# A mask bias moved from TensorE matmuls to a VectorE pass in an attention, and an expert stage of 71 slots instead of 72

## The chip, the cores and the metric

The kernel runs on one core of one Trainium2 chip. The metric is the device time of one execution in microseconds; before the change it is 3022.76 us, the median of three runs (3021.39 to 3025.53).

## The reference

The model has two layers over an activation x of 8 batches of 512 tokens of 512 numbers (4096 tokens, 32 tiles of 128). Each layer is a cross attention to a context of 77 keys per batch, and a feed-forward part:

```python
x = x + cross_attention_0(context, layernorm(x), mask)   # 16 heads of 32, masked softmax over 77 keys
x = x + bit_linear_ffn(layernorm(x))                     # 8-bit activations, ternary weights, a depthwise conv
x = x + cross_attention_1(layernorm(x), context)         # 16 heads of 64, no mask
x = x + moe(layernorm(x))                                # 8 experts, the best 2 per token
```

In the first attention the scores of a masked key are replaced by -1e20 before the softmax; the mask is an input of [8, 1, 512, 77] and is 0 for the padded keys of a batch. The softmax is taken over energy / sqrt(512). In the last part each token goes to 2 of 8 experts, so there are 8192 rows to be worked on, sorted by expert; an expert computes silu(x W_gate) * (x W_up) with 1024 hidden numbers, and multiplies by W_2.

## The kernel before, in words

The program is a sequence of blocks, each finished by all engines before the next begins: the context's keys and values, the first attention, the feed-forward part, the second attention, the routing, the experts, and the combination. The change touches the second, the fifth to seventh through one constant, and the loop of the sixth.

**The first attention** (`attention0`, from L314) goes over 32 tiles of 128 tokens, one per step, software-pipelined by hand: the order in which each engine does its work is written out in its own loop over steps, and semaphores tie them. Heads are worked in two halves of 8; a half's scores are [128, 2, 4 x 77] in two PSUM banks, 616 numbers per token. In step s TensorE does, in this order: for each half the scores of tile s (`score_half`), the mix of values of tile s - 2 (`mix`), the transposes of tile s + 1's normalized input (`turn`), the output product of tile s - 3 (`output`), and the four groups of transposes of tile s - 1's probabilities (`flip`). `score_half` first writes the mask's bias, 0 or -1e20, into PSUM with two matmuls of an identity against the bias row repeated over four heads (L423, 308 columns each, bf16), and then adds 16 small products of 32 rows against 77 keys (L428, fp32). `mix`, `turn` and the `flip`s share a ring of three PSUM banks that ScalarE empties.

VectorE in a step: `add` of tile s - 4 (the output product added to x at L572 and statistics at L574), then `shift` for both halves of tile s (a maximum per head straight from PSUM, L552, and the subtraction from PSUM into SBUF tile `e`, L556), every fourth step `masks` for the next batch (L545), and `invert` for both halves (the sum of exponentials, L565, and its reciprocal, L567). ScalarE in a step: the copy of the mix (L519), the exponential of half 0 (L502), the copy of the turned input (L497), the exponential of half 1, the normalization of tile s + 2 (L489), and the four copies of flipped probabilities (L510). GpSimd multiplies the exponentials by the reciprocals (L397, two of them per tile), adds the output bias to x (L400), and at tile 8 issues one DMA that fills `sorted_x` with zeros. TensorE may write a half's scores again when `shifted` says that the subtraction of the tile before has been done; and it waits for `bias_made` before the scores of a batch's first tile.

**Routing and experts.** `SLOTS` (L1467) is the number of slots of 128 rows in the sorted scratch arrays `sorted_x` and `sorted_y`: 64 for the 8192 rows and one for each expert, 72. Each expert gets its count of rows rounded up to whole slots, at least one; slots behind the last that is used count as expert 7's and hold zeros. `experts` (from L1797) works on all slots alike. Per slot TensorE makes the gate and up products of half 0 (24 matmuls, L1919), transposes a part of the slot before, makes those of half 1, the output product of the slot before (24 matmuls, L1939), and transposes a part of its own; ScalarE, VectorE and the DMA queue of SyncE follow. `slots` (L1831) writes out slots 0 and 1, loops over 34 pairs, and writes out the last two. GpSimd meanwhile loads and splits the weights of the next experts. Behind the experts, GpSimd gathers each token's two rows from `sorted_y` in the combination.

Of the kernel before, what the change touches and what calls it, by code (L numbers as in the profile page):

```python
# [23 lines left out]
ALU = mybir.AluOpType  # L24
ACT = mybir.ActivationFunctionType
AX = mybir.AxisListType

P = 128
# [285 lines left out]
def attention0(nc, core, keys, values, w):  # L314
# [7 lines left out]
    with ExitStack() as stack:  # L322
# [21 lines left out]
        weights_in = sem("weights_in"); bo_in = sem("bo_in"); mask_in = sem("mask_in")  # L344
        variance_ready = sem("variance_ready"); root_ready = sem("root_ready"); steps = sem("steps")
        xn_made = sem("xn_made"); bias_made = sem("bias_made"); bo_added = sem("bo_added")
        scores_ready = sem("scores_ready"); topped = sem("topped"); shifted = sem("shifted")
        exp_done = sem("exp_done"); summed = sem("summed"); inverted = sem("inverted")
        probs_ready = sem("probs_ready"); unit_ready = sem("unit_ready"); unit_copied = sem("unit_copied")
        out_ready = sem("out_ready"); out_added = sem("out_added"); stats_made = sem("stats_made")  # L350
# [22 lines left out]
        def grouped(a):  # L373

            return a.rearrange("p (g h k) -> p g h k", g=2, h=CH)
# [27 lines left out]
        @block.tensor  # L403
        def _(pe):
            def ring_free(u):
                if u >= len(ring):
                    pe.wait_ge(unit_copied, u - len(ring) + 1)

            def turn(t):
                u = unit["turn", t]  # L410
                pe.wait_ge(xn_made, t + 1)
                ring_free(u)
                for k in range(KD):
                    last = nc.tensor.transpose(bank(u)[:, k * P:(k + 1) * P], xn[:, t % 2, k * P:(k + 1) * P],
                                               core.ident[:, :])
                last.then_inc(unit_ready, 1)

            def score_half(t, half):
                b = t // TPS
                if t >= 1:  # L420
                    pe.wait_ge(shifted, 2 * (t - 1) + half + 1)
                for g in range(2):
                    nc.tensor.matmul(scores[half][:, g, 0:QUARTER], core.ident_bf[:, :],  # L423
                                     bias[:, t, :].unsqueeze(1).broadcast_to([P, CH, KEYS]), start=True, stop=False)
                for c in range(CH):
                    for g in range(2):
                        rows = slice((2 * half + g) * DH, (2 * half + g + 1) * DH)
                        last = nc.tensor.matmul(scores[half][:, g, c * KEYS:(c + 1) * KEYS],  # L428
                                                xn_t[rows, t % 2, c, :], keys[rows, c, b * KEYS:(b + 1) * KEYS],
                                                start=False, stop=(c == CH - 1))  # L430
                last.then_inc(scores_ready, 1)

            def flip(t, q):
                u = unit["flip", t, q]
                pe.wait_ge(probs_ready, 2 * t + q // 2 + 1)
                ring_free(u)
                for c in range(CH):
                    last = nc.tensor.transpose(bank(u)[0:KEYS, c * P:(c + 1) * P],
                                               heads(e[:, t % 2, q // 2, :])[:, q % 2 * CH + c, :], core.ident[:, :])
                last.then_inc(unit_ready, 1)  # L440

            def mix(t):
                u = unit["mix", t]
                pe.wait_ge(unit_copied, unit["flip", t, ROWS_OF - 1] + 1)
                ring_free(u)
                for c in range(CH):
                    for j in range(ROWS_OF):
                        last = nc.tensor.matmul(bank(u)[j * DH:(j + 1) * DH, c * P:(c + 1) * P],
                                                values[:, t // TPS, c * P + j * DH:c * P + (j + 1) * DH],
                                                probs_t[:, t % 2, j * CH + c, :], start=True, stop=True)  # L450
                last.then_inc(unit_ready, 1)

            def output(t):
                pe.wait_ge(unit_copied, unit["mix", t] + 1)
                if t >= 1:
                    pe.wait_ge(out_added, t)
                for c in range(CH):
                    last = nc.tensor.matmul(out[:, :], mixed_t[:, t % 2, c, :], wo[:, c, :],
                                            start=(c == 0), stop=(c == CH - 1))
                last.then_inc(out_ready, 1)  # L460

            turn(0)
            for step in range(NT + 3):
                if step < NT:
                    pe.wait_ge(unit_copied, unit["turn", step] + 1)
                    pe.wait_ge(bias_made, step // TPS + 1)
                    for half in range(2):
                        score_half(step, half)
                if step == 3:
                    pe.wait_ge(weights_in, 16)  # L470
                if 2 <= step < NT + 2:
                    mix(step - 2)
                if step + 1 < NT:
                    turn(step + 1)
                if step >= 3:
                    output(step - 3)
                if 1 <= step <= NT:
                    for q in range(ROWS_OF):
                        flip(step - 1, q)
# [61 lines left out]
        def _(dve):  # L541
# [5 lines left out]

            def shift(t, half):
                raw = scores[half][:, :, 0:QUARTER].rearrange("p g (h k) -> p g h k", h=CH)
                tops = top[:, half, :].rearrange("p (g h) -> p g h", g=2)  # L550
                dve.wait_ge(scores_ready, 2 * t + half + 1)
                nc.vector.tensor_reduce(tops, raw, AX.X, ALU.max).then_inc(topped, 1)  # L552
                dve.wait_ge(topped, 2 * t + half + 1)
                if t >= 2:
                    dve.wait_ge(unit_ready, unit["flip", t - 2, 2 * half + 1] + 1)
                nc.vector.tensor_tensor(grouped(e[:, t % 2, half, :]), raw,  # L556
                                        tops.unsqueeze(3).broadcast_to([P, 2, CH, KEYS]), ALU.subtract
                                        ).then_inc(shifted, 1)

            def invert(t, half):  # L560
                sums = total[:, t % 2, half, :]
# [902 lines left out]
CW = 1024  # L1464
CHUNKS = (KD * 2 * MID + MC * D) // CW

SLOTS = (2 * B * S) // P + EXPERTS  # L1467
ROWS = SLOTS * P


# [326 lines left out]
def experts(nc, core, plan, w, sorted_x, sorted_y):  # L1797
# [5 lines left out]
    with ExitStack() as stack:  # L1803
# [27 lines left out]
        def slots(engine, slot):  # L1831

            slot(0, 0, True, False)
            slot(1, 1, False, False)
            with engine.Fori(1, PAIRS - 1) as pair:
                slot(2 * pair, 0, False, False)
                slot(2 * pair + 1, 1, False, False)
            slot(SLOTS - 2, 0, False, False)
            slot(SLOTS - 1, 1, False, True)

        @block.gpsimd
        def _(pool):
# [46 lines left out]
        def _(sp):  # L1889
# [16 lines left out]

            slots(sp, slot)
            for u in range(2):
                sp.wait_ge(y_out[u], 16 * PAIRS)

        @block.tensor
        def _(pe):
# [52 lines left out]
        def _(act):  # L1965
# [11 lines left out]
            def slot(s, u, first, last):  # L1977
                gates(s, 0)
                gates(s, 1)
                if not first:  # L1980
                    out_copy(s - 1, 1 - u)

            slots(act, slot)
            out_copy(SLOTS - 1, 1)

        @block.vector
        def _(dve):
# [139 lines left out]
```

## Time and profile before

| | us |
|---|---|
| median of three runs | 3022.76 (3021.39 to 3025.53) |
| the profiled execution's own time | 3018.94 |
| its span, first to last instruction | 3017.2 |
| first attention, from its first instruction to the last of TensorE's output products | 97.4 to 426.3 |
| experts, first product to last output copy | 1732.1 to 2918.6 |

TensorE's mean granted clock over the span is 0.919 of 2.4 GHz. In the rows, PE is TensorE's matmuls, PEld its weight loads, DVE is VectorE, ACT is ScalarE, POOL is GpSimd and SP is SyncE; a line of the timeline merges like instructions (the xN at its end) and gives the start, the time from the first start to the last end, the line and operation, and in brackets the engine's idle time before it. Matmul ends are modelled, so a busy PE is not a PE at its peak; the starts of weight loads are the better marks of its pace.

### The profile page before, as it was taken

To read this page: it belongs to the slowest core of one execution; us is meant where nothing else is said; L and a number is where in the kernel's file an instruction comes from. 1 tells how busy PE (TensorE), PEld (TensorE's weight loads), DVE (VectorE), ACT (ScalarE), POOL (GpSimd) and SP (SyncE) were. 2 spreads that over 40 slices of the span, in tenths; PEclk is the share of its full clock that TensorE was granted. 3 is DMA by queue.
4 is the path that set the end of the run, shared out by engine and by line. 5 is a ranking of instruction groups with operands and counts; after the bars stand their busy time and mean duration, and the time that the engine had idled before them with its cause. 6 is when DMAs were issued, how large, how long until landed. Compare 5 with 4: busy or idle time off the path is not lost. (4 is left out here: it accounts for less than half of the span.)

```text
span 3017.2 us, 45376 instructions
## 1 busy us (share of the span) xinstructions
PE 2468.1 (82%) x15846; PEld 1309.2 (43%) x16027; DVE 1620.3 (54%) x2256; ACT 1015.7 (34%) x1664; POOL 972.8 (32%) x803
## 2 busy tenths in 40 slices
PE   8799964566666699999982099999999999999960
PEld 5566631222222265556551044444444444444430
DVE  4566668898998465656656332242433424332235
ACT  2355535778885444444343211111111111111100
POOL 0243322677776211111103600060533505320026
PEclk9899986888887899999996599999999999999985
DMA  6350010000000200000024501141322413221128
GB/s 232 117 219 34 2 57 0 1 0 1 0 0 0 73 10 10 14 10 10 6 72 141 198 25 35 33 112 35 104 77 79 115 35 102 79 64 33 35 77 275
DMA packets 154415, 190.30 MB, mean 63 GB/s; under 512 B 100070, under 2 KB 103142, under 8 KB 153782
## 3 DMA queue, kind: packets, MB, share of 16 engines
q1 hardware_dynamic: 128933, 98.44, 11.1%
q0 software_dynamic: 25360, 90.21, 9.2%
q8 instruction: 81, 1.33, 0.2%
q14 instruction: 41, 0.33, 0.0%
HBM read 101.77 MB, written 67.96 MB: 56 GB/s over the span
## 5 line engine op out<-in xcount | busy, mean ns | idle before, releaser
L1919 PE MATMUL e_gate_up<-weights,e_x_t 128*128 x3382 | 760.7, 379 | 122.6 <-DMA e_x_t<-sorted_x 118.7
L1919 PEld LDWEIGHTS e_gate_up<-weights,e_x_t 128*128 128x128 bf16 x3456 | 332.6, 98 | 494.2 <-issue 121.1
L1992 DVE TENSOR_TENSOR e_mid<-e_gate,e_gate_up 128x512 f32<-128x512 f32 x144 | 99.0, 688 | 605.5 <-ACT e_gate L1969 605.5
L1939 PE MATMUL e_out<-weights,e_mid_t 128*128 x1692 | 382.8, 379 | 3.0 <-DVE e_mid_t L2005 1.1
L1969 ACT ACTIVATE e_gate<-e_gate_up 128x512 f32<-128x512 f32 x144 | 86.0, 598 | 721.7 <-PE e_gate_up L1919 721.7
L1939 PEld LDWEIGHTS e_out<-weights,e_mid_t 128*128 128x128 bf16 x1728 | 169.1, 98 | 204.8 <-issue 1.2
L708 POOL TENSOR_TENSOR a_e<-a_e,a_total 128x616 f32<-128x616 f32 x64 | 76.5, 1216 | 451.5 <-DVE a_total L960 451.5
L1135 POOL TENSOR_TENSOR f_shared<-f_shared 128x512 f32<-128x512 f32 x128 | 180.8, 1413 | 125.4 <-DVE f_shared L1413 125.4
L1205 PE MATMUL f_out<-f_w,hidden 128*128 128x512 f16 x512 | 141.9, 404 | 95.1 <-ACT hidden L1307 94.5
L1124 POOL TENSOR_TENSOR hidden<-hidden,f_up_row 128x512 f32<-128x512 f32 x128 | 178.7, 1407 | 86.6 <-ACT f_up_row L1336 86.6
L1873 POOL TENSOR_TENSOR e_token<-e_token 1x1 f32<-1x1 f32 x6 | 1.1, 183 | 632.3 <-PE e_out L1939 632.3
L2005 DVE COPY e_mid_t<-e_mid_flip 128x1024 bf16<-128x1024 bf16 x144 | 98.9, 688 | 180.0 <-PE e_mid_flip L1929 179.4
L736 PE MATMUL a_ring<-a_xn_t,a_wq 128*128 128x512 bf16 x752 | 168.6, 381 | 7.5 <-issue 6.7
L1184 PE MATMUL f_product<-f_xq_t,f_w 128*128 128x512 bf16 x489 | 144.0, 423 | 35.5 <-DVE f_padded L1381 22.3
L790 PE MATMUL a_out<-a_wo,a_mixed_t 128*128 128x512 bf16 x737 | 164.3, 379 | 4.5 <-issue 3.0
L1413 DVE SCALAR_TENSOR_TENSOR f_shared<-f_padded,f_conv_w,f_shared 128x512 f32<-128x512 f32 x128 | 152.2, 1191 | 12.9 <-ACT f_shared L1290 12.5
L1880 POOL TENSOR_TENSOR weights<-raw_weights,weights 128x1024 bf16<-128x1024 f32 x72 | 155.6, 2162 | 6.1
L1975 ACT ACTIVATE e_y_rows<-e_out 128x512 f32<-128x512 f32 x72 | 43.0, 597 | 340.4 <-PE e_out L1939 340.4
L2037 POOL DMA_INDIRECT o_y<-sorted_y,plan_rows x64 | 67.9, 1060 | 276.6 <-PEq L2023 257.4
L397 POOL TENSOR_TENSOR a_e<-a_e,a_total 128x616 f32<-128x616 f32 x64 | 76.4, 1215 | 192.3 <-DVE a_total L567 192.3
L1998 DVE TENSOR_TENSOR e_mid_parts<-e_mid,e_mid_parts 128x512 bf16<-128x512 f32 x144 | 128.5, 892 | 5.0
L930 DVE SCALAR_TENSOR_TENSOR a_query<-a_ring,a_bq,a_query 128x512 bf16<-128x512 f32 x64 | 48.0, 751 | 142.8 <-ACT a_query L847 142.8
(233 smaller groups left out, 3985.3 us busy)
## 6 DMA issues: line engine op xcount, KB each, us to landing
raw_weights<-in_w POOLq DMA_DIRECT2D x72, 512.0 KB, 4.0
sorted_x<-a_zero_row POOLq DMA_DIRECT2D x1, 18432.0 KB, 56.7
sorted_y<-e_y_rows SPq DMA_DIRECT2D x72, 256.0 KB, 2.1
raw_weights<-in_w SPq DMA_DIRECT2D x24, 512.0 KB, 3.7
x<-in_x SPq DMA_DIRECT2D x4, 2048.0 KB, 21.1
out<-x SPq DMA_DIRECT2D x32, 256.0 KB
hidden<-in_w_t SPq DMA_DIRECT2D x1, 4096.0 KB, 17.9
f_shared<-in_w_t SPq DMA_DIRECT2D x1, 4096.0 KB, 13.3
```

What stands on the lines that cost most here:

```text
L736: last = nc.tensor.matmul(bank(u)[:, :], wq[:, a, k, c * P:(c + 1) * P], xn_t[:, d, k, :], start=(k == 0 and a == d == 0), stop=(k == KD - ...
L790: last = nc.tensor.matmul(out[:, :], mixed_t[:, t % 2, a, c, :], wo[:, d, c, :], start=(c == 0 and a == d == 0), stop=(c == CH - 1 and (a, ...
L1124: nc.gpsimd.tensor_tensor(hidden[:, j, :], hidden[:, j, :], up2_row[:, :], ALU.mult).then_inc(scaled_up, 1)
L1135: nc.gpsimd.tensor_tensor(y[:, j % BUF, :], y[:, j % BUF, :], side[:, j % BUF, :], ALU.add).then_inc(right_added, 1)
L1184: last = nc.tensor.matmul(product[j % 2][:, :], w1[:, k, j % HC * P:(j % HC + 1) * P], xq_t[:, parity, k, :], start=(k == 0), stop=(k == K ...
L1205: last = nc.tensor.matmul(out[i][:, :], hq[:, j, i * P:(i + 1) * P], w2[:, j, :], start=False, stop=(j == HC - 1))
L1413: nc.vector.scalar_tensor_tensor(y[:, j % BUF, :], padded[:, j % BUF, 0:S], conv_w[:, j, 0:1], y[:, j % BUF, :], ALU.mult, ALU.add).then_i ...
L1880: nc.gpsimd.tensor_tensor(parts[1], plan.raw[:, n % 2, :], parts[0], ALU.subtract).then_inc(split, 1)
L1919: last = nc.tensor.matmul(gate_up[half][:, part, :], x_t[:, u, a, k, :], plan.weights13[:, bass.ds(expert % 2, 1), b, k, col:col + 512], s ...
L1939: last = nc.tensor.matmul(out[:, :], mid_t[:, a, j, :], plan.weights2[:, bass.ds(expert % 2, 1), b, j, :], start=(j == 0 and a == b == 0), ...
L1992: nc.vector.tensor_tensor(mid[:, half, :], gate[:, half, :], gate_up[half][:, 1, :], ALU.mult).then_inc(mid_made, 1)
L1998: nc.vector.tensor_tensor(mid_parts[:, half, 1, :], mid[:, half, :], mid_parts[:, half, 0, :], ALU.subtract).then_inc(mid_low, 1)
```

## The change

In `score_half` the bias matmuls are gone, and each score product starts a PSUM group of its own. `shift` has three passes for a half instead of two: the bias is added from PSUM into `e`, the maximum is taken from `e`, and the subtraction reads and writes `e`. TensorE's wait for PSUM is now on `biased`, the first of the three, and the wait for `bias_made` is VectorE's. The wait for the transposes of tile t - 2, which frees `e`, stands ahead of the first pass. `SLOTS` becomes 71, so `PAIRS` becomes 35: the loop runs over 33 pairs, three slots are written out behind it, and the last slot has buffer 0.

```diff
--- before.py
+++ after.py
@@ -344,7 +344,7 @@
         weights_in = sem("weights_in"); bo_in = sem("bo_in"); mask_in = sem("mask_in")
         variance_ready = sem("variance_ready"); root_ready = sem("root_ready"); steps = sem("steps")
         xn_made = sem("xn_made"); bias_made = sem("bias_made"); bo_added = sem("bo_added")
-        scores_ready = sem("scores_ready"); topped = sem("topped"); shifted = sem("shifted")
+        scores_ready = sem("scores_ready"); biased = sem("biased"); topped = sem("topped"); shifted = sem("shifted")
         exp_done = sem("exp_done"); summed = sem("summed"); inverted = sem("inverted")
         probs_ready = sem("probs_ready"); unit_ready = sem("unit_ready"); unit_copied = sem("unit_copied")
         out_ready = sem("out_ready"); out_added = sem("out_added"); stats_made = sem("stats_made")
@@ -418,16 +418,13 @@
             def score_half(t, half):
                 b = t // TPS
                 if t >= 1:
-                    pe.wait_ge(shifted, 2 * (t - 1) + half + 1)
-                for g in range(2):
-                    nc.tensor.matmul(scores[half][:, g, 0:QUARTER], core.ident_bf[:, :],
-                                     bias[:, t, :].unsqueeze(1).broadcast_to([P, CH, KEYS]), start=True, stop=False)
+                    pe.wait_ge(biased, 2 * (t - 1) + half + 1)
                 for c in range(CH):
                     for g in range(2):
                         rows = slice((2 * half + g) * DH, (2 * half + g + 1) * DH)
                         last = nc.tensor.matmul(scores[half][:, g, c * KEYS:(c + 1) * KEYS],
                                                 xn_t[rows, t % 2, c, :], keys[rows, c, b * KEYS:(b + 1) * KEYS],
-                                                start=False, stop=(c == CH - 1))
+                                                start=True, stop=True)
                 last.then_inc(scores_ready, 1)
 
             def flip(t, q):
@@ -463,7 +460,6 @@
             for step in range(NT + 3):
                 if step < NT:
                     pe.wait_ge(unit_copied, unit["turn", step] + 1)
-                    pe.wait_ge(bias_made, step // TPS + 1)
                     for half in range(2):
                         score_half(step, half)
                 if step == 3:
@@ -547,15 +543,19 @@
 
             def shift(t, half):
                 raw = scores[half][:, :, 0:QUARTER].rearrange("p g (h k) -> p g h k", h=CH)
-                tops = top[:, half, :].rearrange("p (g h) -> p g h", g=2)
+                now = e[:, t % 2, half, :]
                 dve.wait_ge(scores_ready, 2 * t + half + 1)
-                nc.vector.tensor_reduce(tops, raw, AX.X, ALU.max).then_inc(topped, 1)
-                dve.wait_ge(topped, 2 * t + half + 1)
                 if t >= 2:
                     dve.wait_ge(unit_ready, unit["flip", t - 2, 2 * half + 1] + 1)
-                nc.vector.tensor_tensor(grouped(e[:, t % 2, half, :]), raw,
-                                        tops.unsqueeze(3).broadcast_to([P, 2, CH, KEYS]), ALU.subtract
-                                        ).then_inc(shifted, 1)
+                if t % TPS == 0 and half == 0:
+                    dve.wait_ge(bias_made, t // TPS + 1)
+                nc.vector.tensor_tensor(grouped(now), raw, bias[:, t, :].unsqueeze(1).unsqueeze(1).broadcast_to(
+                    [P, 2, CH, KEYS]), ALU.add).then_inc(biased, 1)
+                dve.wait_ge(biased, 2 * t + half + 1)
+                nc.vector.tensor_reduce(top[:, half, :], heads(now), AX.X, ALU.max).then_inc(topped, 1)
+                dve.wait_ge(topped, 2 * t + half + 1)
+                nc.vector.tensor_tensor(heads(now), heads(now), top[:, half, :].unsqueeze(2).broadcast_to(
+                    [P, HALF, KEYS]), ALU.subtract).then_inc(shifted, 1)
 
             def invert(t, half):
                 sums = total[:, t % 2, half, :]
@@ -1464,7 +1464,7 @@
 CW = 1024
 CHUNKS = (KD * 2 * MID + MC * D) // CW
 
-SLOTS = (2 * B * S) // P + EXPERTS
+SLOTS = (2 * B * S) // P + EXPERTS - 1
 ROWS = SLOTS * P
 
 
@@ -1835,8 +1835,9 @@
             with engine.Fori(1, PAIRS - 1) as pair:
                 slot(2 * pair, 0, False, False)
                 slot(2 * pair + 1, 1, False, False)
-            slot(SLOTS - 2, 0, False, False)
-            slot(SLOTS - 1, 1, False, True)
+            slot(SLOTS - 3, 0, False, False)
+            slot(SLOTS - 2, 1, False, False)
+            slot(SLOTS - 1, 0, False, True)
 
         @block.gpsimd
         def _(pool):
@@ -1906,7 +1907,7 @@
 
             slots(sp, slot)
             for u in range(2):
-                sp.wait_ge(y_out[u], 16 * PAIRS)
+                sp.wait_ge(y_out[u], 16 * (PAIRS + 1 - u))
 
         @block.tensor
         def _(pe):
@@ -1981,7 +1982,7 @@
                     out_copy(s - 1, 1 - u)
 
             slots(act, slot)
-            out_copy(SLOTS - 1, 1)
+            out_copy(SLOTS - 1, (SLOTS - 1) % 2)
 
         @block.vector
         def _(dve):
```

## Rows read from the trace of the kernel before

**Rows 1.** The page, busy time of each engine over the whole span.

```profile
PE 2468.1 (82%) x15846; PEld 1309.2 (43%) x16027; DVE 1620.3 (54%) x2256; ACT 1015.7 (34%) x1664; POOL 972.8 (32%) x803
```

**Rows 2.** Windows: length, busy by engine (instructions), granted clock (PEclk), DMA share, GB/s.

```profile
97.00:121.00 24.00, 15.45 (x96) 12.04 (x96) 12.16 (x30) 10.22 (x14) 4.61 (x5) 0.51 0.82 283
...
207.15:399.51 192.36, 192.36 (x1922) 133.41 (x1921) 130.57 (x204) 100.11 (x180) 72.45 (x61) 1.00 0.14 52
...
440.00:960.00 520.00, 303.37 (x1253) 131.37 (x1276) 461.69 (x449) 380.68 (x600) 328.91 (x238) 0.83 0.00 1
...
1030.00:1550.00 520.00, 492.15 (x4628) 299.41 (x4672) 308.96 (x486) 224.35 (x379) 77.17 (x68) 0.99 0.04 9
...
1732.00:2918.00 1186.00, 1178.98 (x6226) 571.83 (x6334) 405.64 (x576) 128.47 (x216) 276.59 (x226) 1.00 0.23 62
```

**Rows 3.** Timeline, first attention, one step of TensorE: start us, us, instructions.

```profile
207.15 0.21 PEld L423 LDWEIGHTS a_scores<-a_bias,ident_bf 128*128 128x128 bf16 x2
...
207.62 0.97 PEld L428 LDWEIGHTS a_scores<-keys,a_xn_t 32*128 32x128 f32 x16 [0.27 <-issue]
...
208.67 0.12 PEld L423 LDWEIGHTS a_scores<-a_bias,ident_bf 128*128 128x128 bf16 x2
...
209.05 0.97 PEld L428 LDWEIGHTS a_scores<-keys,a_xn_t 32*128 32x128 f32 x16 [0.27 <-issue]
...
210.10 0.81 PEld L448 LDWEIGHTS a_ring<-a_probs_t,values 77*32 77x32 f32 x32
...
216.78 0.21 PEld L423 LDWEIGHTS a_scores<-a_bias,ident_bf 128*128 128x128 bf16 x2
```

**Rows 4.** The same timeline and step, VectorE.

```profile
208.79 0.80 DVE L552 TENSOR_REDUCE a_top<-a_scores 128x8 f32<-128x616 f32 x1 [1.69 <-PE a_scores L428]
...
209.62 0.80 DVE L556 TENSOR_TENSOR a_e<-a_scores,a_top 128x616 f32<-128x616 f32 x1
...
210.34 0.79 DVE L552 TENSOR_REDUCE a_top<-a_scores 128x8 f32<-128x616 f32 x1
...
212.48 0.79 DVE L565 TENSOR_REDUCE a_total<-a_e 128x8 f32<-128x616 f32 x1 [0.52 <-ACT a_e L502]
...
213.57 0.79 DVE L565 TENSOR_REDUCE a_total<-a_e 128x8 f32<-128x616 f32 x1
...
215.31 0.69 DVE L572 TENSOR_TENSOR x<-x,a_out 128x512 f32<-128x512 f32 x1 [0.71 <-PE a_out L458]
...
216.03 0.69 DVE L574 BATCH_NORM_STATS2 stats<-x 128x6 f32<-128x512 f32 x1
```

**Rows 5.** The same timeline and step, ScalarE and GpSimd.

```profile
212.83 0.72 ACT L502 ACTIVATE a_e<-a_e 128x616 f32<-128x616 f32 x1
...
213.43 0.81 ACT L489 ACTIVATE a_xn<-x,shift,rstd 128x512 f32<-128x512 f32 x1
...
213.59 2.39 POOL L397 TENSOR_TENSOR a_e<-a_e,a_total 128x616 f32<-128x616 f32 x2 [6.00 <-DVE a_total L567]
...
215.68 2.05 ACT L510 ACTIVATE a_probs_t<-a_ring 77x512 f32<-77x512 f32 x4 [1.43 <-PE a_ring L438]
215.94 1.28 POOL L400 TENSOR_TENSOR x<-x,a_bo 128x512 f32<-128x512 f32 x1
```

**Rows 6.** Single lines: VectorE passes with two SBUF operands, ns min/median/max.

```profile
L1998 DVE TENSOR_TENSOR e_mid_parts<-e_mid,e_mid_parts x144: 691/693/2498, 1740.5 to 2907.3; 128x512 bf16<-128x512 f32 x144
...
L1413 DVE SCALAR_TENSOR_TENSOR f_shared<-f_padded,f_conv_w,f_shared x128: 736/1168/1765, 490.4 to 960.3; 128x512 f32<-128x512 f32 x128
```

**Rows 7.** Timeline, start of the first attention: the mask, and step 3 of TensorE.

```profile
105.52 0.32 DVE L545 TENSOR_SCALAR a_bias<-a_mask 128x308 bf16<-128x308 int32 x1 [5.12 <-DMA a_mask<-in_mask]
...
130.21 0.21 PEld L423 LDWEIGHTS a_scores<-a_bias,ident_bf 128*128 128x128 bf16 x2
```

**Rows 8.** Timeline, experts: the first products of the last two slots.

```profile
2877.98 4.90 PEld L1919 LDWEIGHTS e_gate_up<-weights,e_x_t 128*128 128x128 bf16 x24
...
2894.42 4.90 PEld L1919 LDWEIGHTS e_gate_up<-weights,e_x_t 128*128 128x128 bf16 x24
```

## The prediction

> **What bounds the kernel now.** I read the page's busy times first [rows 1]: TensorE is busy 82% of the span, VectorE 54%. That is a mean over unlike stages, so I then cut the span into windows [rows 2]. The chain of waits is no help here: it follows back only through the last 95 us, the combination behind the experts. What the reader is to see in the windows: in the steady part of the first attention TensorE's records leave no gap at all (192.36 of 192.36 us) while VectorE is busy 130.57, or 68%; in the experts TensorE is busy 1178.98 of 1186, or 99%. Both stages that the change touches are TensorE's, at a granted clock of 1.00 (the 2.4 GHz level). Then the timeline of one attention step, one engine at a time [rows 3 to 5], gives the pace and the slack of the others.
>
> The pace: TensorE runs 96 matmuls per tile (4 bias, 32 score products in both halves, 32 mix, 4 turn, 8 output, 16 flip), so 1922 in the window are 20 steps, of 192.36 / 20 = 9.62 us; the two bias loads of neighbouring steps are 9.63 apart [rows 2, 3].
>
> **Part 1: TensorE without the bias matmuls.** From the first bias load of half 0 to its first score load is 207.62 - 207.15 = 0.47 us; for half 1 it is 209.05 - 208.67 = 0.38 [rows 3]. The scores themselves keep a pitch of 1.05 per half (207.62 to 208.67, 209.05 to 210.10), with or without the bias. So a step loses at most 0.85. Some of the 0.47 of half 0 is the change-over from the transposes before it, which the first score load will then have to make; the lower bound is 0.65, if it keeps 0.2 of it. I take 0.75, twice the 0.375 of half 1, where nothing but the bias stands between two runs of scores. In a sentence by itself: the Trainium skill (TensorE: Matmul & The Clock Gate, Back-to-back issue gap) gives a warm matmul of N columns N / 2.4 + 2.5 ns, by which four of 308 columns would be an estimated 0.52 us, and the sum below would be 6.6 us smaller. The row is taken instead because it holds the 0.27 us of issue that the trace shows behind each bias pair [rows 3]. New period of TensorE: 9.62 - 0.75 = 8.87.
>
> Starting each score group afresh instead of adding to the bias changes no instruction count or shape; I cost it at nothing, since the overwriting products of `mix` run under it at no worse pitch (32 in the 0.81 us and a little, from 210.10) [rows 3].
>
> **Part 2: VectorE's third pass.** The bias add reads one PSUM and one SBUF operand of 616 numbers into fp32, as the subtraction does now: 0.80 us. The maximum moves from PSUM to SBUF: the sum of exponentials has that shape from SBUF, at 0.79, against 0.80. The subtraction now has both operands in SBUF; alone, such a pass takes what a pass from PSUM takes (691 ns for 512 numbers at the least [rows 6], against 0.69 for the add of x [rows 4]). With the pitches of the timeline [rows 4]: a pass that waits for the one before follows in 0.83 (208.79 to 209.62), one that does not in 0.72 (209.62 to 210.34). Half: 0.83 + 0.83 + 0.72 = 2.38; two halves 4.76. The two sums with their reciprocals 2 x 1.09 (212.48 to 213.57) = 2.18. The add and the statistics 0.72 + 0.69 = 1.41. A quarter of the mask's 0.32 [rows 7] is 0.08. Together 8.43 per step, where now it is 6.77. That is under 8.87 by 0.44, so the 1.66 us of new work per step are hidden under TensorE, and VectorE is then about 95% busy. If that cover fails it costs what VectorE's period exceeds 8.87.
>
> Is its order right for that? I lay the new step on the old marks, with 0 at the first score load of tile s. Half 0's scores are ready at 208.79 - 207.62 = 1.17. The shifts run to 5.9 or 6.0. The exponential of half 1 ends about 6.8, the normalization (0.81) at 7.5; the first flip copy is due at the old 215.68 - 207.62 = 8.06 less half 1's 0.38, 7.7 [rows 5]. So ScalarE, in whose queue the four flip copies stand behind that exponential, is in time by 0.2: that is the thinnest margin here. Sums and reciprocals run 5.95 to 8.1, the add (its output product ended with 215.31 - 207.62 = 7.69, less 0.38) to 9.5; the next scores are ready at 8.87 + 1.17 = 10.0. VectorE's waits of now (1.69 + 0.52 + 0.71 = 2.92 of the step, [rows 4]) are what pays for the new pass. GpSimd's multiplies move to 7.0 to 9.4 and their readers on TensorE come a whole step later, at 15.9: over 6 us to spare.
>
> **Waits that move.** TensorE's wait for PSUM is on the first pass of the tile before, 8 us ahead of need. The wait for `bias_made` moves from TensorE to VectorE. At the head this lets the scores of tile 0 go before the mask has landed (105.52 [rows 7]); the mask then holds VectorE, with the shifts and behind them ScalarE's exponential queued. Laying out the first steps with the half-clock that the head has (0.51 in 97 to 121 [rows 2]), VectorE's passes and ScalarE's order take back most of it, and step 3 starts at about 128.9 instead of 130.21 [rows 7]: 1.3 us gained, with bounds of 0 (VectorE holds all of it) and 3 (the whole early start is kept).
>
> **Part 3: one slot less.** The products of the last two slots start 2894.42 - 2877.98 = 16.44 us apart [rows 8], and 1186 / 72 is 16.5 [rows 2]. A slot has the same instructions whether its rows are real or zeros, so one slot less is 16.4 off TensorE's chain. With it go one transposing load and one store on SyncE's queue, two gates and a copy on ScalarE, eight passes on VectorE, all beside TensorE. Written-out slots run no slower than looped ones: both starts above are of written-out slots, and the pitch is that of the mean, so the third one behind the loop costs nothing. The last slot's buffer is 0 and SyncE waits for 36 and 35 stores: no new wait. The zero fill shrinks by 1/72, hidden in the first attention.
>
> **Sum.** 28 periods from step 3 to step 31 and step 31's own bias: 29 x 0.75 = 21.8; head 1.3; slot 16.4. In all 39.5. The profiled execution's own time, 3018.94 (span 3017.2), would be 2979.4. It lies 3.8 below the median of the runs, 3022.76; against that I predict 2983.3, say 2983. The terms' bounds: 29 x 0.65 to 29 x 0.85 is 18.9 to 24.7, head 0 to 3, slot 16.4 to 16.5: 35.3 to 44.2 less, 2978.6 to 2987.5.
>
> **Rivals.**
> (a) VectorE becomes the bound of the first attention at a period between 8.87 and 9.62. For it: only 0.44 us of slack on 8.43 and 0.2 on ScalarE's order. Against: every duration is that of a row of the same shape. At 9.3 the attention gains 29 x 0.32 = 9.3, and with the slot and the head 27: about 2996.
> (b) The attention gains nothing and only the slot pays: 3022.8 - 16.4 = 3006. It needs 1.2 us of unforeseen work or waits in each step.
> (c) The other side. VectorE's subtraction has, for the first time in this stage, two SBUF operands, and such passes are stretched where GpSimd works beside them: 1168 ns in the median and 736 at the least in the ffn, where GpSimd is busy 63% of the window, and up to 2498 against 691 in the experts [rows 2, 6]. If each of the two subtractions waited out one of GpSimd's multiplies (2.39 / 2 = 1.2 us [rows 5]), VectorE's step would be 8.43 + 2.4 = 10.83, 1.21 over the present 9.62; 29 of them are 35 us lost, less 16.4: 3041. It decides against the kernel from 9.62 + 16.4 / 29 = 10.19 on, 1.76 us of waits per step. The Trainium skill (SBUF — State Buffer, SBUF: two separate sides) states this as a lock: a VectorE pass with two SBUF inputs and a GpSimd pass that reads SBUF exclude each other for a whole instruction. By that rule, the rows' long maxima agree. Against it here: GpSimd's work follows the first reciprocal and lasts to 217.22 - 213.59 = 3.6 us behind it [rows 5], so from 7.0 to 10.7 on my scale, and the first subtraction of the next tile starts at 8.87 + 1.17 + 1.66 = 11.7. They miss each other by 1.0 us; even with VectorE as the bound by 0.4.
> (d) The slot doesn't pay: TensorE's last slot is at the end of the chain, with 99% busy before it, so I see no way but a slower slot (code of a third written-out slot, addresses): about 2999.
> A clock rival I fold into (a): where TensorE is busy 58% the granted clock is 0.83 and where it is 95% it is 0.99 [rows 2]; a TensorE that waits for VectorE by 0.4 in 9.3 stays near the second.
>
> **How the numbers follow.** The forecast 0.72, (a) 0.14, (b) 0.05, (c) 0.04, (d) 0.05. The predicted time is the forecast's, 2983. The range goes from 2976 (the lower bound less the runs' own scatter of some 2 us) to 2996, which takes in (a) up to a period of 9.3; outside remain part of (a), (b), (c) and (d), under 0.2. A measurement of this kernel can tell some 0.2%, 6 us, from no change. All cases but (c) are over that: faster 0.95, same 0.01, slower 0.04.
>
> **What would show it.** Right: score loads of neighbouring tiles 8.87 apart at a clock of 1.00; no gap in TensorE's records in the steady part; VectorE busy 95% there, the new add at 0.80, the subtraction at 0.80 with no long ones; step 3 at about 129; the experts' first product to their last output copy 16.4 shorter. Wrong: waits of ScalarE's or TensorE's on `shifted` in every step, with TensorE idle before the flips (a); subtractions of 1.2 to 2 us beside GpSimd's multiplies (c); an expert slot over 16.5 us (d).

## The result, and the profile after

The changed kernel takes 2971.91 us (median of four runs, 2970.4 to 2973.19) against 3022.07 for the kernel before: a ratio of 0.9836, 95% interval 0.9819 to 0.9853, so 50 us less. The forecast was 2983, with a range of 2976 to 2996: the direction was right, and the gain, put at 39.5, was larger than the range allowed. The profiled executions differ by 47.7 us (2971.29 with a span of 2969.5, against 3018.94 with 3017.2).

The table cuts the span at the starts of the first VectorE pass of each block's normalization, of the experts' first weight load and of their last output copy, in us (the last column is what lies before the first cut and behind the last):

| profile | attention 1 | ffn | attention 2 | routing | experts | ends |
|---|---|---|---|---|---|---|
| before | 331.0 | 574.6 | 544.7 | 184.1 | 1186.2 | 196.6 |
| changed | 301.7 | 571.7 | 545.8 | 184.7 | 1169.6 | 196.0 |
| difference | -29.3 | -2.9 | +1.1 | +0.6 | -16.6 | -0.6 |

The page of the changed kernel, beside [rows 1]:

```profile
span 2969.5 us, 44895 instructions
...
PE 2414.8 (81%) x15632; PEld 1277.5 (43%) x15811; DVE 1654.8 (56%) x2312; ACT 1016.7 (34%) x1661; POOL 972.4 (33%) x803
```

Its windows, beside [rows 2]: the head, 15 steps of the first attention, and the experts.

```profile
97.00:121.00 24.00, 13.52 (x98) 11.44 (x98) 15.78 (x35) 12.08 (x18) 7.61 (x7) 0.50 0.84 283
207.70:337.35 129.65, 128.15 (x1383) 89.26 (x1382) 116.98 (x185) 77.20 (x136) 54.31 (x46) 1.00 0.17 62
1701.40:2871.00 1169.60, 1162.29 (x6140) 564.02 (x6248) 400.66 (x568) 126.58 (x212) 276.67 (x226) 1.00 0.23 63
```

The experts show what was forecast: one slot less, 16.6 us. In the steady attention 1383 matmuls at 92 to the tile are 15 steps of 8.64 us, where 8.87 was forecast and 9.62 it was; VectorE is busy 90% there, and TensorE's records now have gaps (128.15 of 129.65). One step on the timeline, beside [rows 3 to 5]:

```profile
207.70 1.49 PEld L425 LDWEIGHTS a_scores<-keys,a_xn_t 32*128 32x128 f32 x32 [0.16 <-ACT a_probs_t L506]
...
208.86 0.80 DVE L552 TENSOR_TENSOR a_e<-a_scores,a_bias 128x616 f32<-128x616 f32 x1 [0.67 <-PE a_scores L425]
209.26 0.81 PEld L445 LDWEIGHTS a_ring<-a_probs_t,values 77*32 77x32 f32 x32
...
210.53 0.80 DVE L557 TENSOR_TENSOR a_e<-a_e,a_top 128x616 f32<-128x616 f32 x1
...
212.90 0.80 DVE L557 TENSOR_TENSOR a_e<-a_e,a_top 128x616 f32<-128x616 f32 x1
...
213.61 0.79 DVE L565 TENSOR_REDUCE a_total<-a_e 128x8 f32<-128x616 f32 x1
213.73 0.72 ACT L498 ACTIVATE a_e<-a_e 128x616 f32<-128x616 f32 x1 [1.17 <-DVE a_e L557]
...
214.35 0.80 ACT L485 ACTIVATE a_xn<-x,shift,rstd 128x512 f32<-128x512 f32 x1
214.43 0.20 DVE L567 RECIPROCAL a_total<-a_total 128x8 f32<-128x8 f32 x1
214.55 0.75 DVE L565 TENSOR_REDUCE a_total<-a_e 128x8 f32<-128x616 f32 x1
...
215.06 2.02 ACT L506 ACTIVATE a_probs_t<-a_ring 77x512 f32<-77x512 f32 x4
...
215.46 0.65 DVE L572 TENSOR_TENSOR x<-x,a_out 128x512 f32<-128x512 f32 x1
215.74 0.43 PEld L435 LDWEIGHTS a_ring<-ident,a_e 128*77 128x77 f32 x4 [0.30 <-issue]
...
216.34 1.49 PEld L425 LDWEIGHTS a_scores<-keys,a_xn_t 32*128 32x128 f32 x32 [0.16 <-ACT a_probs_t L506]
```

Two things are new. The 32 score products of a tile take 1.56 us (207.70 to 209.26), not the 2 x 1.05 of [rows 3]. By the starts of single loads half 1 begins 0.52 us after half 0 (208.21 and 207.70), when ten of half 0's sixteen products have gone, and from there the two alternate. And the last four flips are late: their loads wait 0.30 us. The profile names no releaser; my reading is that they wait until ScalarE's first flip copy, which begins at 215.06, has emptied a bank, and experiment 4 tests it.

The subtraction with two SBUF operands, all 64 of the changed kernel (ns min/median/max), is never stretched:

```profile
L557 DVE TENSOR_TENSOR a_e<-a_e,a_top x64: 799/799/801, 107.6 to 376.9; 128x616 f32<-128x616 f32 x64
```

### The profile page after: what moved, and what is told of

Read it like the earlier page. It is cut to its first block and busy times, and to the rows that moved or that the text cites. A ratio compares the mean times of both kernels' runs of the same rounds, so it can differ in the third digit from the quotient of the medians.

```text
span 2969.5 us, 44895 instructions
## 1 busy us (share of the span) xinstructions
PE 2414.8 (81%) x15632; PEld 1277.5 (43%) x15811; DVE 1654.8 (56%) x2312; ACT 1016.7 (34%) x1661; POOL 972.4 (33%) x803
## 5 line engine op out<-in xcount | busy, mean ns | idle before, releaser
L1920 PE MATMUL e_gate_up<-weights,e_x_t 128*128 x3335 | 749.9, 379 | 122.0 <-DMA e_x_t<-sorted_x 118.2
```

The source lines that it names most:

```text
L1920: last = nc.tensor.matmul(gate_up[half][:, part, :], x_t[:, u, a, k, :], plan.weights13[:, bass.ds(expert % 2, 1), b, k, col:col + 512], s ...
```

## The experiments

**1 and 2. Each part alone.** The first is the changed kernel with `SLOTS` and its loop as before, the second the kernel before with 71 slots. The line that differs, as it stands in the second (not shown: the loop's last slots and SyncE's counts, which follow it):

```diff
-SLOTS = (2 * B * S) // P + EXPERTS
+SLOTS = (2 * B * S) // P + EXPERTS - 1
```

> The changed kernel with 72 slots, so the attention's part of the change alone. My theory: it holds all of the gain but a slot. In the changed kernel's trace the first attention ends 29.2 us earlier (428.41 to 399.21) and the experts from their first weight load to their last output copy are 16.6 us shorter. Theory: span about 2986, step period 8.64, experts 1186. Rival, the two parts help each other (the stages behind the attention come out shorter for another reason, since 1.9 us of the span's 47.7 are in stages that the change does not touch): then the span is off 2986 by more than 2 us.

> The kernel before with 71 slots and nothing else. Theory: 16.4 to 16.6 us less than before, all of it in the experts, span about 3001. Rival: the stages in between (the ffn was 2.9 us shorter and the second attention 1.2 us longer in the changed kernel's trace) move here too, by 1 to 3 us either way; then those are scatter between programs and no effect of the mask's bias.

Measured: 2990.31 us for the bias alone (0.9899 of before, 0.9883 to 0.9916) and 3005.55 for the slot alone (0.9950, 0.9934 to 0.9967), where the kernel before, run beside them, took 3019.08. These medians are 28.8 and 13.5 us less, 42.3 together, against 50.2 for the whole; the two ratios multiply to 0.985, which the intervals don't tell from 0.9836. By stage the parts are what the whole was: attention 302.0 with a period of 8.65 and experts 1186.9 in the first; experts 1169.8 in the second. But the spans, 2991.8 and 3004.9, are 5.8 and 3.9 us above what I expected, which by the letter is the first rival's outcome. No interaction is seen, though: what is off lies in code that is the same. In the first the second attention took 547.8 and the ends 197.4. In that attention the granted clock was at its lower level for one long stretch (0.50 in the window 1016 to 1039.8, where the changed kernel has 0.78 at the same distance from the stage's start); that this cost the 2 us is likely but not tested, and the ends stay unexplained. In the second the first attention took 334.2, 3.2 more than in the profile of before with the same code there. A window of that profile shows why: the granted clock is 0.57, where the kernel before had 1.00 from 120.5 us on, and the step in it took 12.85 us instead of 9.62.

```profile
132.00:140.00 8.00, 8.00 (x62) 5.45 (x61) 5.19 (x8) 2.99 (x5) 1.81 (x3) 0.57 0.00 0
```

**3. The same bias matmuls, in another place.** On the kernel before. `bias_half` is the wait for PSUM and the two bias matmuls, taken out of `score_half` as they stand (not shown); `score_half` keeps the products.

```diff
+                    for half in range(2):
+                        bias_half(step, half)
                     for half in range(2):
                         score_half(step, half)
```

> The kernel before, with the four bias matmuls of a tile ahead of all 32 score products instead of two ahead of each half. Same work, same 72 slots. Theory: the two halves use rows 0 to 63 and rows 64 to 127 of the array and run side by side where no full-array matmul stands between them, as in the changed kernel's trace (32 products in 1.56 us from 207.70 to 209.26, against 2 x 1.05 before). Then the step period falls from 9.62 to 8.97 to 9.08 and the time by 16 to 20 us. Rival: the products were slow because they added to what lies in PSUM, and are fast when they overwrite; then both halves still take 2.1 us together and the time falls by 3 us at most (one change-over less).

Measured: 3003.04 us, 0.9944 (0.9927 to 0.9960), attention 313.7, period 8.99. TensorE's weight loads:

```profile
203.68 0.48 PEld L422 LDWEIGHTS a_scores<-a_bias,ident_bf 128*128 128x128 bf16 x4
204.43 1.49 PEld L430 LDWEIGHTS a_scores<-keys,a_xn_t 32*128 32x128 f32 x32 [0.27 <-issue]
206.00 0.81 PEld L450 LDWEIGHTS a_ring<-a_probs_t,values 77*32 77x32 f32 x32
...
212.67 0.48 PEld L422 LDWEIGHTS a_scores<-a_bias,ident_bf 128*128 128x128 bf16 x4
```

All products still add to the bias in PSUM, and the 32 take 1.57 us. So it isn't overwriting that made them fast: the two halves run side by side as soon as nothing over the full array stands between them. 0.63 us of every step of the kernel before (9.62 - 8.99) were the place of the bias matmuls and not their work: 0.53 of it is the products' (2.10 to 1.57), and the other 0.10 goes with one change-over less between bias and products.

**4. The normalization out of ScalarE's way.** On the changed kernel:

```diff
                 if step < NT:
                     exponential(step, 1)
-                if step + 2 < NT:
-                    norm(step + 2)
                 if 1 <= step <= NT:
                     for q in range(ROWS_OF):
                         flipped(step - 1, q)
+                if step + 2 < NT:
+                    norm(step + 2)
```

> The changed kernel with one thing more: ScalarE normalizes tile t + 2 after the four flip copies instead of before them. Theory: the changed kernel's period of 8.64 is a loop: scores, VectorE's two shifts, the exponential of half 1, the normalization (0.71 us of pitch), the first flip copy, the fourth group of flips that needs its bank, the next scores; TensorE itself needs only 8.23. With the normalization out of the loop the two waits before the fourth flips (0.30) and the next scores (0.16) go, the period is 8.23 to 8.3 and the time 10 to 12 us under the changed kernel's. Rival: VectorE (about 8 us of work per step) or GpSimd sets the period, then it stays at 8.6.

Measured: 2965.46 us, 0.9818 (0.9802 to 0.9834), attention 295.6, period 8.44: 6 to 7 us under the changed kernel, not 10 to 12.

```profile
202.50 1.77 PEld L435 LDWEIGHTS a_ring<-ident,a_e 128*77 128x77 f32 x15 [0.28 <-issue]
...
203.13 2.04 ACT L506 ACTIVATE a_probs_t<-a_ring 77x512 f32<-77x512 f32 x4 [0.39 <-PE a_ring L435]
...
204.43 1.49 PEld L425 LDWEIGHTS a_scores<-keys,a_xn_t 32*128 32x128 f32 x32 [0.16 <-ACT a_probs_t L506]
...
206.00 0.81 PEld L445 LDWEIGHTS a_ring<-a_probs_t,values 77*32 77x32 f32 x32
...
212.88 1.26 PEld L425 LDWEIGHTS a_scores<-keys,a_xn_t 32*128 32x128 f32 x28 [0.16 <-ACT a_probs_t L506]
```

The flips' loads run through (202.50 to 204.27) and ScalarE's copy now waits for TensorE, not TensorE for it; the loop was real. What I had missed is in the next line: between the last flip load and the first score load stand 0.16 us in every kernel without the bias matmuls. TensorE's need is 8.44 and not 8.23, so the loop had cost 0.20 us a step.

**5, 9 and 10. The same kernels again**, unaltered, for the 1.8 us that had gone from stages that the change doesn't touch.

> The changed kernel once more, unaltered. Theory: the 5 us by which the stages that the change does not touch differ between the profiles so far (1498.2 us in the changed kernel's, 1500.0 in the kernel before's, 1499.0 to 1503.0 in three experiments) is scatter from execution to execution, so here the first attention takes 301.7 to 302 again and the experts 1169.6 to 1170, while the rest lands anywhere from 1498 to 1503, and the median is 2971 to 2976. Rival: the rest is a fixed property of each program; then it is 1498.2 within 0.3.

> The kernel before, unaltered. The ffn, whose code no kernel here changes, took 574.6 us in the profile of before, 571.7 and 571.6 in the two of the changed kernel, and 573.4 to 575.0 in the others. Theory: it depends on where in the chip's own rhythm of clock changes the ffn begins, so on the execution and not on the mask's bias; then one more profile of before lies anywhere from 571.5 to 575. Rival: it belongs to the program; then it is 574.6 within 0.3. The first attention should take 331.0 and the experts 1186.2 to 1186.9 in any case.

> The changed kernel a third time, for the same question. Theory of the rhythm: the ffn takes anything from 571.5 to 575. Rival of the program: 571.6 or 571.7 again.

Measured, by stage:

| profile | attention 1 | ffn | attention 2 | routing | experts | ends | span |
|---|---|---|---|---|---|---|---|
| changed, again | 302.1 | 571.6 | 545.6 | 184.0 | 1169.9 | 195.1 | 2968.3 |
| changed, third | 302.0 | 571.7 | 545.4 | 183.5 | 1170.3 | 194.7 | 2967.5 |
| before, again | 332.5 | 571.8 | 545.5 | 185.5 | 1187.4 | 196.5 | 3019.2 |

The times: 2972.17 for the changed kernel again (median of four, 0.9842, 0.9826 to 0.9859), and 2969.25 and 3020.98 for the single runs of the changed kernel's third and of before. The changed kernel's untouched stages sum to 1496.3 us in the second profile (2968.3 - 302.1 - 1169.9) and to 1495.2 in the third, under 1498.2 and under the range I had given too. The kernel before had an ffn of 571.8 this time: its 574.6 did not belong to the program, and nothing shows that the 2.9 us are an effect of the change. That the ffn goes by where it starts in the rhythm of the clock is not shown either; three profiles of the changed kernel agree to 0.1 us, which is the outcome that I had given the rival of experiment 10. All three sums of the changed kernel lie under both of the kernel before (1500.0 and 1499.3), but experiment 1, with the same attention, had 1502.9: a small effect on these stages is neither shown nor excluded. The first attention (332.5) and the experts (1187.4) of the kernel before are not the 331.0 and 1186.2 to 1186.9 that I had called certain. One step of that attention took 11.26 us instead of 9.62, and the granted clock is 0.79 in the window 132 to 140 around it: the same fall as in experiment 2, in the kernel before itself.

**6. A separator put in.** On top of experiment 4:

```diff
                 if t >= 1:
                     pe.wait_ge(biased, 2 * (t - 1) + half + 1)
+                if half == 1:
+                    nc.tensor.matmul(scores[1][:, 1, 511:512], core.ident_bf[:, :], core.ident_bf[:, 0:1],
+                                     start=True, stop=True)
```

> The kernel with the late normalization, and ahead of half 1's score products one bf16 matmul of one column over the full array, into a column of PSUM that nobody reads. It adds next to no work of its own (one column). Theory of the separator: the two halves of the array can no longer run side by side, so a tile's 32 products take 2.1 us again instead of 1.57, and since this kernel's first attention is bound by TensorE at 8.44 the period goes to 8.95 to 9.1. Rival: what the bias matmuls cost was their columns alone; then the period stays at 8.44 to 8.5.

Measured: 2989.02 us, attention 319.2, period 9.08.

```profile
202.50 0.97 PEld L428 LDWEIGHTS a_scores<-keys,a_xn_t 32*128 32x128 f32 x16 [0.16 <-ACT a_probs_t L509]
203.54 0.10 PEld L423 LDWEIGHTS a_scores<-ident_bf 128*128 128x128 bf16 x1
203.65 0.97 PEld L428 LDWEIGHTS a_scores<-keys,a_xn_t 32*128 32x128 f32 x16
204.70 0.81 PEld L448 LDWEIGHTS a_ring<-a_probs_t,values 77*32 77x32 f32 x32
...
211.58 0.97 PEld L428 LDWEIGHTS a_scores<-keys,a_xn_t 32*128 32x128 f32 x16 [0.16 <-ACT a_probs_t L509]
```

One column over the full array costs 0.64 us a step (9.08 - 8.44). The products take 2.20 us with it (202.50 to 204.70), 1.57 without. With experiment 3 this shows it from both sides. Both separators, this one and the bias, were bf16 besides going over the full array, among fp32 products of 32 rows; which of the two ends the overlap was not tried. The attention's 319.2 also holds three steps of 10.7 us in which the clock fell for some 3 us each (0.57 in the window 289 to 293), so the period is the figure to compare.

**7. GpSimd kept busy beside the subtraction.** On the changed kernel (not shown: the tile `extra` and its semaphore):

```diff
+                nc.gpsimd.tensor_tensor(extra[:, 0, :], bo[:, :], bo[:, :], ALU.mult).then_inc(extra_made, 1)
+                pool.wait_ge(extra_made, 2 * t + 1)
+                nc.gpsimd.tensor_tensor(extra[:, 1, :], bo[:, :], extra[:, 0, :], ALU.mult).then_inc(extra_made, 1)
+                pool.wait_ge(extra_made, 2 * t + 2)
```

> The changed kernel, with two needless multiplies of 512 numbers per tile on GpSimd behind its addition to x, on tiles that nothing else uses. GpSimd's work then reaches into VectorE's first subtraction of the next tile, which has two SBUF operands. Theory (the prediction's rival (c) needs an overlap that the change does not have): the first subtraction of a tile stretches from 0.80 to 1.2 to 2 us, the second stays at 0.80, and the period grows from 8.64 by what the first has lost, to 8.9 to 9.8. Rival: passes with two SBUF operands do not mind GpSimd in this stage; then all subtractions stay at 0.80 and the period at 8.64.

Measured: 2982.29 us, attention 308.6. From the timeline, and then the two lines by themselves (ns min/median/max):

```profile
203.34 1.04 POOL L402 TENSOR_TENSOR a_extra<-a_bo 128x512 f32<-128x512 f32 x1
...
204.45 1.29 POOL L404 TENSOR_TENSOR a_extra<-a_bo,a_extra 128x512 f32<-128x512 f32 x1
...
205.25 1.15 DVE L562 TENSOR_TENSOR a_e<-a_e,a_top 128x616 f32<-128x616 f32 x1
...
213.44 1.04 POOL L402 TENSOR_TENSOR a_extra<-a_bo 128x512 f32<-128x512 f32 x1
...
214.24 0.89 DVE L562 TENSOR_TENSOR a_e<-a_e,a_top 128x616 f32<-128x616 f32 x1
...
214.55 1.73 POOL L404 TENSOR_TENSOR a_extra<-a_bo,a_extra 128x512 f32<-128x512 f32 x1
```

```profile
L562 DVE TENSOR_TENSOR a_e<-a_e,a_top x64: 799/821/1335, 107.4 to 383.7; 128x616 f32<-128x616 f32 x64
...
L404 POOL TENSOR_TENSOR a_extra<-a_bo,a_extra x32: 1275/1722/1735, 116.9 to 390.2; 128x512 f32<-128x512 f32 x32
```

First subtractions now take 0.8 to 1.2 us, mostly 0.89 or 1.12, and nearly all second ones still 0.80; GpSimd's second pass takes 1.72, against 1.28 at the least.

The lines show who waits. Of two passes that meet, the one that started first keeps its length, and the later one is longer by what was left of the first, less some 0.14 us. At 205.25 GpSimd's pass has 0.49 to go (204.45 + 1.29), and the subtraction takes 0.35 more than 0.80. At 214.24 the first extra pass has 0.24 to go (213.44 + 1.04), and the subtraction takes 0.09 more; at 214.55 that subtraction has 0.58 to go (214.24 + 0.89), and GpSimd's pass takes 0.45 more than 1.28. In all meetings of a subtraction and a GpSimd pass in this trace the difference is 0.12 to 0.15. So the Trainium skill's lock (SBUF — State Buffer, SBUF: two separate sides), by which the one that starts first has the port for its whole instruction and the other waits, agrees with this trace but for those 0.14 us.

So the contention of rival (c) exists, and here it is cheap because the passes barely meet. The period is 8.74 in most steps and 8.97 in every fourth, under the 8.9 to 9.8 that I expected: 0.10 and 0.33 over 8.64, which is what the subtraction lost (0.09 and 0.32). The attention took 6.9 us more than the changed kernel's 301.7; some 2 of them are in two steps, one of 9.48 in which the second subtraction met a pass too, and one of 10.06 in which the clock fell (0.57 in the window 194 to 198). The changed kernel meets it once, at the head: GpSimd's addition of tile 1 takes 1.85 us instead of 1.27, behind a subtraction that had started 0.09 earlier. From then on its GpSimd is done in time: in the step above the addition ends at 209.69, and the subtraction starts at 210.53.

**8. Four row groups at a time.** On top of experiment 4 (not shown: TensorE waits once for both halves of `biased`, and tells VectorE of each half behind its own last product):

```diff
-                for c in range(CH):
-                    for g in range(2):
-                        rows = slice((2 * half + g) * DH, (2 * half + g + 1) * DH)
+                for c in range(CH):
+                    for half in range(2):
+                        for g in range(2):
+                            rows = slice((2 * half + g) * DH, (2 * half + g + 1) * DH)
```

> The kernel with the late normalization, and a tile's 32 score products in another order: for each of the four chunks all four row groups, instead of one half's two row groups for all chunks and then the other's. Theory: four row groups run side by side, the 32 products take 0.9 to 1.1 us instead of 1.57, TensorE needs about 7.9 us per tile, and the bound becomes VectorE's 8 us of passes (or its loop with ScalarE, about the same): period 8.0 to 8.1, and 9 to 13 us less than the kernel with the late normalization alone (2965). Rival: TensorE's pace in these products is set by issue or by loads, not by which rows they use; then the period stays at 8.44.

Measured: 2952.65 us (2950.54 to 2954.66), 0.9778 (0.9762 to 0.9794), attention 281.7, period 7.94. It beats both kernels; against the changed one it is 19 us less.

```profile
207.59 0.98 PEld L426 LDWEIGHTS a_scores<-keys,a_xn_t 32*128 32x128 f32 x32 [0.16 <-ACT a_probs_t L507]
...
208.10 0.69 DVE L575 BATCH_NORM_STATS2 stats<-x 128x6 f32<-128x512 f32 x1
...
208.65 0.81 PEld L447 LDWEIGHTS a_ring<-a_probs_t,values 77*32 77x32 f32 x32
...
208.76 0.80 DVE L553 TENSOR_TENSOR a_e<-a_scores,a_bias 128x616 f32<-128x616 f32 x1
...
213.51 0.32 DVE L542 TENSOR_SCALAR a_bias<-a_mask 128x308 bf16<-128x308 int32 x1
...
215.53 0.65 PEld L426 LDWEIGHTS a_scores<-keys,a_xn_t 32*128 32x128 f32 x20 [0.16 <-ACT a_probs_t L507]
```

The 32 products take 1.06 us. VectorE goes from the statistics straight into the next tile (208.10, 208.76) and TensorE's loads have no gap either: both need 7.94, and in most steps which of them binds isn't told apart. But every fourth period is 8.11, and it is the one behind the mask pass (213.51), which adds work to VectorE alone: TensorE's last four flips, which follow without a gap in the other steps, wait 0.27 us there (at 223.05). So VectorE's chain binds in that step.

## Why the prediction was wrong

- **The slot: right.** 16.4 forecast, 16.6 measured in the changed kernel (1186.2 to 1169.6), 16.4 in the slot alone.
- **Part 1, TensorE without the bias matmuls, is the step that failed.** "The scores themselves keep a pitch of 1.05 per half, with or without the bias" took from rows with a separator what holds only with it. TensorE's need fell by 9.62 - 8.44 = 1.18 a step, not 0.75. The products' own pace gave 0.53 of it (2.10 to 1.57 for the 32), which the prediction had at nothing; the bias pairs and their change-overs gave the other 0.65, the prediction's lower bound for them, since the change-over from the flips to the products stays (0.16). Told apart by the experiments, the place of the bias matmuls cost 0.63 (experiment 3) and their work 8.99 - 8.44 = 0.55. That last figure is close to the 0.52 that the Trainium skill's gap per matmul (TensorE: Matmul & The Clock Gate, Back-to-back issue gap) gave, so for the work alone the page was nearer than my 0.75. The Trainium skill says of small matmuls in distinct row groups that they run concurrently (TensorE: Matmul & The Clock Gate, Part 3: Packing small matmuls — row/col tiling), and the runs agree: the same 32 products take 2.1 (before) or 2.2 us (experiment 6) with a separator between the halves, 1.57 with the halves next to each other (experiment 3), where four row groups work for a part of the time, and 1.06 with all four in turn (experiment 8).
- **Part 2, VectorE: right in kind, too dear.** The three passes cost what the rows said (4.75 us, forecast 4.76), and were hidden. The sums with reciprocals were put at 2.18 and take 1.85 (213.61 to 215.46): the 1.09 read in [rows 4] held a short wait for the exponential. VectorE's step is 7.97 without the mask, where 8.35 was forecast.
- **ScalarE's order: the thin margin was the right place, and it gave way.** In time by 0.2 at a period of 8.87, it was late by 0.2 at TensorE's true need, 8.44. That is why the period is 8.64, and not rival (a)'s bound by VectorE's own work. Net per step: 0.98 instead of 0.75, over 29 steps 28.4 us instead of 21.8.
- **The head: 0.4 instead of 1.3.** The scores of tile 0 did go earlier (103.19 instead of 106.58), but the granted clock stayed at its lower level longer, to 127.3 us (126.7 and 127.1 in experiments 5 and 10), where it was 120.5 before (120.1 in experiment 9). That it is the missing matmuls that held the clock down is not shown: experiment 3 has all of them, and there the clock rose only at 131.5. The window 122 to 127 of the kernel before (granted clock 1.00) and of the changed kernel (0.50):

```profile
122.00:127.00 5.00, 5.00 (x80) 4.12 (x79) 3.10 (x4) 1.86 (x5) 2.57 (x3) 1.00 0.00 0
```

```profile
122.00:127.00 5.00, 5.00 (x59) 4.38 (x56) 4.41 (x6) 1.69 (x3) 0.15 (x1) 0.50 0.01 2
```

- **The rest.** Of the 10.7 us by which the gain of the medians exceeds the forecast, about 6 are the attention, 2.5 lie in where the profiled executions stand to their medians, and 2 in untouched stages, which in experiments 1, 5, 9 and 10 differ by as much between profiles of the same code. Without the last two the gain is 29.3 + 16.6 = 45.9, and 3022.8 - 45.9 = 2976.9 would have been just inside the range; the bounds of the step term, 0.65 to 0.85, were still wrong, since 0.98 was the truth.
- **Rivals.** (b) and (d) did not happen; (c) did not, for the reason that the prediction gives, with 0.84 us between the passes (210.53 - 209.69) where it had 1.0. Experiment 7 shows the wait itself but not (c)'s price, since most subtractions there meet only the last 0.24 us of a GpSimd pass. An estimate from its meetings: a subtraction that starts right behind a multiply's start would lose the multiply's 1.2 less 0.14, so (c)'s 2.4 a step was about right for passes that fully meet.

## What to carry to other kernels

Before pricing a removed instruction by its own length, ask what it kept apart: a full-array matmul between products that use different rows of the array ended their overlap here, even with a single column. Products over few rows belong next to each other, with the row groups alternating. A slack that is read at one period has to be read again at the shorter one. And where VectorE and GpSimd share work, look at which pass starts first and what is left of it when the other starts.

## What the runs showed of the hardware

One bf16 column over the full array between two runs of 16 fp32 products of 32 rows costs 0.64 us. A VectorE subtraction with two SBUF operands and a GpSimd pass that meet do not slow each other evenly: the later one waits out the earlier, less 0.12 to 0.15 us, in every meeting of experiment 7. And the clock can fall for a few us in the steady part with TensorE busy throughout by its records (8.00 of 8.00 us in the window 132 to 140 of experiments 2 and 9, whose first attention is that of before); what brought it down is open. So is what sets the time of its rise in the head, 120.1 to 131.5 us over the profiles named above.
